# Adding expert results, layer norm and transposes inside the second attention's pipeline

## The reference, cut to what matters

```
x = x + tanh(g_xattn[0]) * L0_attention(layernorm(x), ctx)
x = x + tanh(g_ffn[0])   * L0_experts(layernorm(x))      # 16 experts, each row picks 4, plus a shared one
x = x + tanh(g_xattn[1]) * L1_attention(layernorm(x), ctx, ctx, mask)
x = x + tanh(g_ffn[1])   * L1_experts(layernorm(x))      # 8 experts, each row picks 2, plus a shared one
```

```
scores = einsum('bqghd,bkgd->bghqk', Q / 4, K) + slope * (k - q)      # 16 heads of width 16, 4 key groups
w      = softmax(where(mask, scores, lowest))
out    = einsum('bghqk,bkgd->bqghd', w, V).reshape(b, q, 256) @ Wo
```

## Time and profile before

| | us |
|---|---|
| median of 3 runs | 1741.26 (1736.82 to 1741.35) |
| profiled execution | 1740.45 |
| its span | 1738.4 |
| mean granted TensorE clock | 0.946 of 2.4 GHz |
| TensorE busy in the span | 1505.6 (87%) |
| VectorE busy | 1267.0 (73%) |
| ScalarE busy | 1046.5 (60%) |
| GpSimd busy | 794.7 (46%) |

### The profile page before, as it was taken

The page is one execution under the profiler, slowest core; times in us unless marked ns, Lnnn a source line. Parts: engine busy times, 40 slices in busy tenths (PEclk is TensorE's granted clock), DMA queues, the critical chain, the costliest instruction groups (busy, mean ns, idle before and its releaser), DMA issues. The chain is left out here.

```text
span 1738.4 us, 40154 instructions
## 1 busy us (share of the span) xinstructions
PE 1505.6 (87%) x11666; PEld 1166.6 (67%) x11666; DVE 1267.0 (73%) x4783; ACT 1046.5 (60%) x3220; POOL 794.7 (46%) x1224
## 2 busy tenths in 40 slices
PE   0499999999999999999498889991499997699998
PEld 0389888889888889888354467770366665455554
DVE  5589999999999999999576556666565554544444
ACT  4578888888888888888344345550277674222222
POOL 0766666666666666666207734441365652000000
PEclk9999999999999999999788989996599998699999
DMA  7594200000000000000116534435210000000000
GB/s 292 163 216 103 63 0 0 0 0 0 0 0 0 0 0 0 0 0 2 55 29 203 167 115 124 125 116 208 67 31 22 22 22 3 1 1 13 12 12 12
DMA packets 75226, 95.58 MB, mean 55 GB/s; under 512 B 32138, under 2 KB 60298, under 8 KB 73606
## 3 DMA queue, kind: packets, MB, share of 16 engines
q1 hardware_dynamic: 68278, 75.53, 15.1%
q0 software_dynamic: 6864, 19.01, 3.0%
HBM read 62.74 MB, written 40.43 MB: 59 GB/s over the span
## 5 line engine op out<-in xcount | busy, mean ns | idle before, releaser
L673 ACT ACTIVATE prob<-bS,ntop 128x128 f32<-128x128 f32 x512 | 181.5, 369 | 48.4 <-DVE ntop L480 48.4
L577 POOL TENSOR_TENSOR rs<-ve,half 128x6 f32<-128x6 f32 x128 | 177.3, 1385 | 0.0
L453 DVE TENSOR_SCALAR qn<-qn,mv,rs 128x128 f32<-128x128 f32 x512 | 145.9, 347 | 6.3 <-POOL rs L577 4.7
L324 PE MATMUL bS<-kT,qT 128*128 128x128 f32 x1024 | 138.3, 279 | 13.2 <-ACT prob L673 12.9
L585 POOL TENSOR_SCALAR kv<-kv,rs,nb 128x128 f32<-128x128 f32 x256 | 132.3, 522 | 27.5 <-POOL nb L580 27.5
L300 PE MATMUL bq<-w,xq 128*128 128x256 f16 x1024 | 133.8, 274 | 6.7 <-DVE xq L425 6.7
L324 PEld LDWEIGHTS bS<-kT,qT 128*128 128x128 f32 x1024 | 126.1, 194 | 16.8 <-issue 14.3
L644 ACT ACTIVATE qT<-bqT,vecs 128x256 f32<-128x256 f32 x256 | 134.9, 596 | 3.6 <-PE bqT L284 3.6
L574 POOL TENSOR_TENSOR ve<-mv,eps 128x6 f32<-128x6 f32 x128 | 34.9, 273 | 219.7 <-DVE mv L446 219.7
L341 PE MATMUL bO<-pT,kv 128*128 128x256 f32 x512 | 132.0, 380 | 1.9 <-ACT pT L657 1.9
L358 PE MATMUL bY<-wproj,catq 128*128 128x256 f16 x1024 | 132.7, 273 | 0.8 <-DVE catq L500 0.8
(11 more groups left out here) (296 smaller groups left out, 4315.2 us busy)
## 6 DMA issues: line engine op xcount, KB each, us to landing
f_xblk<-by_slot SPq DMA_DIRECT2D x79, 132.0 KB, 2.1
by_slot<-zeros SPq DMA_DIRECT2D x1, 10112.0 KB, 35.8
f_xn<-by_pick SPq DMA_DIRECT2D x16, 512.0 KB, 4.3
f_wstage<-by_expert SPq DMA_DIRECT2D x16, 480.0 KB, 3.6
l_piece<-in_f_w SPq DMA_DIRECT2D x16, 312.0 KB, 2.9
wo_stage<-in_wproj SPq DMA_DIRECT2D x8, 512.0 KB, 4.1
by_expert<-in_f_w SPq DMA_DIRECT2D x18, 128.0 KB, 2.8
x<-in_x SPq DMA_DIRECT2D x1, 2048.0 KB, 8.3
```

The lines of the kernel that those rows point to most:

```text
L324: done = nc.tensor.matmul(bS[:, h, :], qT[:, t, h, :], kT[:, t, h // HPG, :], start=True, stop=True)
L453: done = nc.vector.tensor_scalar(qn[:, off % 4, h, :], qn[:, off % 4, h, :], mv[:, t, h, 0:1], rs[:, t, h:h + 1], ALU.subtract, ALU.mult)
L577: nc.gpsimd.tensor_tensor(rs[:, t, :], ve[:], r["half"][:, 0:6], ALU.pow).then_inc(rs_ready, 1)
L673: done = nc.scalar.activation(prob[:, t, h, :], bS[:, h, :], ACT.Exp, bias=ntop[:, t, h:h + 1], scale=SCALE, accum_out=total[:, t, h:h + 1])
```

## The change

The adding loop leaves `sparse_ffn`, and the stage "a1n" is gone. `attention1` gets both:

- Before its pipeline it splits the small weights, adds the four picks of batches 0 and 1, and normalises, turns and splits batch 0.
- In the loop, while batch b is worked on, VectorE adds the picks of batch b+2 (two in step 0, two in step 1, around find_top), takes its statistics in step 2 ahead of find_top, aggregates them behind find_top, and normalises it in step 3. GpSimd computes its two small scale instructions. In batch b+1's step 0 TensorE turns batch b+2 into the upper half of the PSUM bank of V; ScalarE takes its high part at the end of step 0, VectorE its low part at the start of step 1.
- TensorE's projection of q and k moves from step 0 to step 1, ScalarE's take of it from step 1 to step 2, and VectorE's take of V from step 3 to step 2.
- The two halves of the keys are counted one by one, and TensorE waits for each where it needs it.
- SyncE fetches the picks of batch n+2 behind weight piece n, into two buffers in place of four.

```diff
@@ attention1, TensorE
+            def turn_x(b, u):
+                reach(pe, s["v_ready"], b)
+                reach(pe, x_low, b)
+                pe.wait_ge(x_normed, b + 1)
+                for k in range(KT):
+                    done = nc.tensor.transpose(bv[:, D + k * P:D + (k + 1) * P], xn[:, u, k * P:(k + 1) * P], ident)
+                done.then_inc(x_turned, 1)
...
             def score(b, u, c):
-                if c == 0:
-                    pe.wait_ge(s["kblock_ready"], b + 1)
+                if c % 2 == 0:
+                    pe.wait_ge(s["kblock_ready"], b * 2 + c // 2 + 1)
...
-                if more and c == 0:
+                if ahead and c == 0:
+                    turn_x(b + 1, 1 - u)
+                if ahead and c == 1:
                     project_qk(b + 1)
-                if more and c == 1:
                     project_v(b + 1)
@@ attention1, ScalarE
-                if more and c == 1:
+                if ahead and c == 2:
                     take_qk(b + 1, 1 - u)
                 if live(2):
                     take_pT(b, c - 2)
                 if live(0):
                     exponents(b, u, c)
+                if ahead and c == 0:
+                    take_high(b + 1)
@@ attention1, VectorE
+            def add_pick(b, u, half, k):
+                dve.wait_ge(combined if k else back_loaded[u], b * K0 + k if k else half * 16 + 16)
+                nc.vector.scalar_tensor_tensor(out=x[:, b, :], in0=back[:, u, k, :], scalar=shares[:, b, k:k + 1],
+                                               in1=x[:, b, :], op0=ALU.mult, op1=ALU.add).then_inc(combined, 1)
...
+                if ahead and c == 1:
+                    take_low(b + 1)
                 if live(0):
                     add_alibi(b, c)
+                if ahead > 1 and c < 2:
+                    add_pick(b + 2, u, half + 1, 2 * c)
...
                 if live(4) and c == 2:
                     divide(b - 1)
-                if more and c == 3:
+                if ahead and c == 2:
                     take_v(b + 1, 1 - u)
+                if ahead > 1 and c == 2:
+                    take_stats(b + 2)
                 if live(0):
                     find_top(b, c)
+                if ahead > 1 and c < 2:
+                    add_pick(b + 2, u, half + 1, 2 * c + 1)
+                if ahead > 1 and c == 2:
+                    take_moments(b + 2, u)
+                if ahead > 1 and c == 3:
+                    norm_x(b + 2, u)
@@ attention1, GpSimd
+            def x_scales(b, u):
+                pool.wait_ge(x_moments, b + 1)
+                nc.gpsimd.tensor_tensor(xve[:], xmv[:, u, 1:2], r["eps"][:, 0:1], ALU.add).then_inc(x_ve, 1)
+                pool.wait_ge(x_ve, b + 1)
+                nc.gpsimd.tensor_tensor(xrs[:, u, :], xve[:], r["half"][:, 0:1], ALU.pow).then_inc(x_rs, 1)
...
+            with pool.Fori(1, B // 2 - 1) as i:
+                x_scales(i * 2 + 1, 1)
+                keys_and_piece(i, 0)
+                x_scales(i * 2 + 2, 0)
+                keys_and_piece(i, 1)
@@ attention1, SyncE
+            def load_back(n):
+                reach(sp, combined, (n - 1) * K0)
+                sp.dma_start(back[:, n % 2].rearrange("p k d -> p (k d)"), of_token[n]).then_inc(back_loaded[n % 2], 16)
+            load_back(0)
...
+            load_back(1)
...
+            for n in range(B):
+                reach(sp, s["piece_low"], n - 1)
+                sp.dma_start(piece[:, n % 2, :], w_next[:, n * PIECE:(n + 1) * PIECE]).then_inc(piece_loaded[n % 2], 16)
+                if n + 2 < B:
+                    load_back(n + 2)
```

More of the change, by code:

```diff
@@ L974, in sparse_ffn @@
     STEPS = NC * NS
-    FETCH, BACK = 4, 4
+    FETCH = 4
     HI, LO = 0, HALF
@@ L1702, in turn_p, with step @@
                 done.then_inc(s["p_turned"], 1)
-            def step(b, u, c, live, more):
+            def step(b, u, half, c, live, ahead):
                 if live(0):
@@ L1764, in step @@
                     nc.scalar.copy(oT[:].rearrange("p a b -> p (a b)"), bY[:, 0, :]).then_inc(s["oT_ready"], 1)
+            act.wait_ge(small_loaded, 16 * len(small))
+            at = 0
+            for src, high, low in small:
+                n = src.shape[-1]
+                nc.scalar.activation(high, small_stage[:, at:at + n], ACT.Copy, scale=WS).then_inc(small_high, 1)
+                at += n
+            take_high(0)
             take_qk(0, 0)
@@ L1819, in step @@
                     nc.vector.bn_stats(r["row_stats"][:, b - 2, :], x[:, b - 2, :])
+            at = 0
+            for q, (src, high, low) in enumerate(small):
+                n = src.shape[-1]
+                dve.wait_ge(small_loaded, 16 * len(small))
+                dve.wait_ge(small_high, q + 1)
+                nc.vector.scalar_tensor_tensor(out=low, in0=small_stage[:, at:at + n], scalar=WS, in1=high, op0=ALU.mult,
+                                               op1=ALU.subtract).then_inc(small_low, 1)
+                at += n
+            for k in range(K0):
+                add_pick(0, 0, 0, k)
+            take_stats(0)
+            take_moments(0, 0)
+            add_pick(1, 1, 0, 0)
+            add_pick(1, 1, 0, 1)
+            norm_x(0, 0)
+            add_pick(1, 1, 0, 2)
+            add_pick(1, 1, 0, 3)
+            take_low(0)
+            take_stats(1)
+            take_moments(1, 1)
             take_v(0, 0)
+            norm_x(1, 1)
+            dve.wait_ge(later_loaded, 16 * len(later))
             pipeline(dve, step)
@@ new lines, in keys_and_piece @@
+            def keys_and_piece(i, u):
+                block_keys(i * 2 + u, u)
+                split_piece(i, u)
+            nc.gpsimd.memset(r["ones16"][:], 1.0)
+            pool.wait_ge(mask_loaded, 16)
+            nc.gpsimd.tensor_scalar(r["maskneg"][:].rearrange("p b s -> p (b s)"), mask[:], -1.0, 3.0e38, ALU.add,
+                                    ALU.mult).then_inc(mask_ready, 1)
+            x_scales(0, 0)
+            x_scales(1, 1)
+            keys_and_piece(0, 0)
+            x_scales(2, 0)
@@ L1852, in _ @@
+            keys_and_piece(0, 1)
+            with pool.Fori(1, B // 2 - 1) as i:
[3 more added lines that the diff above has]
+                keys_and_piece(i, 1)
+            x_scales(B - 1, 1)
+            keys_and_piece(B // 2 - 1, 0)
+            keys_and_piece(B // 2 - 1, 1)
         @block.sync
         def _(sp):
[L1854 to L1858, removed]
@@ L1863, in program @@
+            sp.dma_start(mask[:], mask_in).then_inc(mask_loaded, 16)
+            load_back(1)
+            for into, src in later:
+                sp.dma_start(into, src).then_inc(later_loaded, 16)
+            for n in range(B):
[3 more added lines that the diff above has]
+                    load_back(n + 2)
 def program(nc, t, out):
@@ L2093, in program @@
                 small.append((t[name].rearrange("p k n -> p (k n)"), flat2(r[name][0]), flat2(r[name][1])))
[L2095 to L2099, removed]
-                nc.gpsimd.memset(r["ones16"][:], 1.0)
-                pool.wait_ge(later, 48)
-                nc.gpsimd.tensor_scalar(r["maskneg"][:].rearrange("p b s -> p (b s)"), mask[:], -1.0, 3.0e38, ALU.add, ALU.mult)
+            later = ((r["wo1"][:], t["wo1"]), (r["alibi"][:], t["alibi"]))
             mf = Memory(nc, l1)
             weights = ffn_memory(mf, "f1", NT1)
-            normalise(nc, r, "a1n", None, small, load_later, early=0, finish=make_mask)
-            attention1(nc, r, t["f1_w"], weights[0])
+            attention1(nc, r, t["f1_w"], weights[0], small, later, t["mask"], by_pick, shares0)
             ffn(mf, "f1", NT1, weights, gw1, E1, E1, K1, SHARED1, False, 3, out=out)
```

118 lines of the change are left out of this document (69 added, 49 removed).

## The result

The changed kernel takes 1799.96 us (median of 4 runs, 1791.28 to 1802.05); the kernel before took 1740.99 in the same comparison. The ratio is 1.034 (95% interval 1.030 to 1.037): slower, outside the range of the prediction. Ratios compare fast executions alone; one that is over 1.5% above the fastest of its kernel counts as slow. The profiled execution has a span of 1800.0 us and a granted clock of 0.923, against 1738.4 and 0.946.

The account below looks back on a forecast made before the run. The prediction took TensorE to bound the attention loop, with two stages ahead leaving it mostly idle. Paid 55 us (50 in the loop, 5 for the clock) less 48.3 saved is 6.7 more: 1748 us, forecast's own range 1738 to 1758, overall 1724 to 1774.

Parts of the forecast that it names:

- What bounds the kernel: In the second attention's loop, TensorE is the engine the others wait for, with a period of 13.15 us.
- the new wait: Before each next batch's step 0, TensorE stands 2.1 us for keys queued behind GpSimd's scales, in 14 batches; bounds 1.7 and 2.6.
- From the first to the third score, 8.9: In each loop batch, 7.66 us now plus 0.33 for turning and 0.9 for the low part gives 8.9.
- the clock term: Low clock behind the loop's new gaps: 1.2 us each after 4 of 14, 5 us in all; bounds 0 and 17.
- Rival C: In the loop, the clock falls behind each wait, costing 17 us in place of 5: 1760; chance 0.11.
- The low part before the projection, 0.9: In the loop, VectorE's held-up norm delays the low part the projection needs: 0.3 to 1.4 us, taken as 0.9.
- TensorE's added work, 0.33 a batch: In the loop, TensorE gets two more transposes, costing 0.33 us a batch, fully paid.
- Rival D: In step 0, VectorE's adds wait for GpSimd's split, up to 1.3 us a batch, 18 us: 1766; chance 0.12.
- Saved ahead of the pipeline, 48.3: Before the loop, first scores come at 1201.9 in place of 1250.24, saving 48.3 us; bounds 44 and 51.
- the fetch's queueing: Ahead of the pipeline, the small weights queue behind the first 512 KB of the fetch, 0.3 us by estimate.

Follow-up runs that it names:

- Wait alone: Kernel before with moved projections, keys counted by halves and GpSimd's wait for step 2's negated top, without the adding work: 1833.3 us, ratio 1.052.
- wait filled: Kernel before with moved projections and GpSimd's wait, plus 18 unused matmuls where TensorE stood for the keys: 1770.6 us, ratio 1.017.
- h1_both_again: Changed kernel with statistics and moments at the end of step 1, and x turned and its high and low parts taken earlier; rerun undisturbed: 1713.6 us, ratio 0.983.
- the control: Kernel before with moved projections and keys counted by halves, without the adding stage's work or wait in the loop; run again: 1745.5 us, ratio 1.002.
- f3_lowonly: Changed kernel with x turned and its high and low parts taken earlier, statistics and moments left in step 2; beside a disturbed kernel before: 1831.0 us, ratio 1.030.
- early moments: Changed kernel with statistics and moments of batch b+2 moved from step 2 to the end of step 1: 1752.3 us, ratio 1.005.

## Why the prediction was wrong

- **What bounds the kernel, and the place of the new wait: right.** In the loop TensorE stood for the keys 13 times, 24.8 us in sum, 1.90 to 1.93 us each in the steady part (forecast 2.1, 14 times), and 7.67 us passed from the third score to the next batch (7.6).
- **From the first to the third score, 8.9: wrong,** 12.77. Not one instruction was missing from the walk; those from 1354.1 to 1364.4 ran at the lower clock. In the three batches at clock 1.00 it was 9.7.
- **The step that failed is the clock term: "I let 4 of 14 be followed by it, 5 us, with bounds 0 and 14 x 1.2 = 17".** Both halves failed. Nearly every wait was followed by the low clock (in the changed kernel three periods of 17.4 were the exceptions), and for some 10 us, not the 3.4 of the earlier trace rows. Wait alone against wait filled gives 61.3 us for it, 3.6 times the upper bound. In the changed kernel it is, by difference, 294.4 - 212.6 (the loop with neither wait) - 24.8 - 7.0 (the two waits) = 50.0 us. Rival C named the mechanism at 0.11, and the sign set down for it, a loop clock below 0.9, came (0.77); but it had the same mis-sized price.
- **Why the price was too low.** My bound took one low stretch as the price of every gap; that gap lay in another stage, with other work around it. The window of the earlier trace rows also began 1 us behind the start of that stretch and ran 1 us past its end, so even there 1.2 us should have been 1.7. And I had not looked behind the gap of 4.22 us ahead of the first score, in this very stage: the clock was low for the next 5.8 us. Both in the profile before:

```profile
921.60:925.00 3.40, 3.40 (x15) 2.06 (x16) 1.81 (x2) 0.17 (x1) 2.79 (x3) 0.50 0.95 226
1250.30:1256.10 5.80, 5.80 (x28) 3.52 (x29) 1.55 (x3) 1.56 (x9) 3.66 (x3) 0.50 0.13 27
```

- **The low part before the projection, 0.9:** in the changed kernel hardly seen, since TensorE was late itself; in the three batches at clock 1.00 it was 1.5, and with the keys' wait gone 1.6 a batch. I had priced a second chain as an addition to the first. It is a floor under it.
- **TensorE's added work, 0.33 a batch:** no run shows it alone. The floor with no wait is 14.15, not 13.48. The moved projections give 5.7 us over the loop. Of the 7 more, short waits of TensorE account for about 4 (5.6 us in h1_both_again's loop, 2.1 of them for the norm, against 1.7 in the control); the rest I can't name.
- **Rival D, the adds wait for GpSimd: wrong in its time, right in its mechanism.** In the changed kernel the adds' median is 480 ns; three of 64 took over 0.8 us, the longest 1.03, and in the steady loop the first add of a batch took 0.52, since it came when GpSimd's instruction had 0.24 us to go. Where the order put an add just behind the start of GpSimd's instruction, as in f3_lowonly, it took 1.54 us in 11 batches and ended 0.3 us after that instruction:

```profile
1376.83 1.36 POOL L1926 TENSOR_TENSOR f_w<-l_piece,f_w 128x624 f32 x1 [0.17 <-POOL l_piece L1924]
1376.94 1.54 DVE L1825 SCALAR_TENSOR_TENSOR x<-l_back,shares,x 128x256 f32 x1
```

By the Trainium skill, page "SBUF — State Buffer", section "Who interferes with whom", such instructions contend with GpSimd's reads; these rows agree.
- **Saved ahead of the pipeline, 48.3: 41.2,** below my bound of 44. The walk lacked the drain: SyncE had seen the stores at 1186.8, as counted, and the block's first instruction came at 1191.85, where the walk had 1186.9, 4.9 later. Data and split took 1.3 more; the fetch's queueing, 0.3 by my estimate, is not seen by itself.

The loop's 99.5 us are thus 17.7 without any of the waits, 24.8 and 7.0 of standing and 50.0 of clock. Less 41.2 saved, with 3.7 ahead of the change and -0.4 behind the loop, that is the 61.6 us between the spans.

## What to carry to other kernels

Where TensorE has no slack, price a new wait by where it sits: here 1.9 us of standing took another 4 by the clock in the mean of the batches, so a wait in a loop is to be designed away, or filled, before its length matters. When one wait is removed look for the next chain that was hidden by it; here the gain came only when both were gone. And what stands at a block's boundary (a drain, a barrier) is free only as long as another stage covers it.

## What the runs showed of the hardware

- Behind an idle time of 1.9 us TensorE's first score ran on at 2.4 GHz, then came 10 us of work at 1.2 GHz, in most batches; behind 1.5 us (early moments) it was 3.4 us of each 17, but in the filled version of the changed kernel waits of the same length were followed by it in only 6 of 15 batches. Work of 2.1 us in the same place, its result unused, kept the granted clock at 1.00. That a kernel gets 63 us faster (1833.3 to 1770.6) by adding matmuls was new to me.
- GpSimd's drain at the end of the block that ends in indirect DMAs takes 8.04 to 8.07 us in every profile here, counted from its own record, which begins 0.6 us ahead of that of the last issue. Where nothing else held the block (the profile after and six more), GpSimd's first instruction came 6.8 us behind the end of that issue.
- VectorE's instructions beside GpSimd's: the norm took 2.06 us beside the keys, and 0.40 in the mean of 12 with the early moments, where it began within 0.1 us of the end of GpSimd's instruction. VectorE's adds, whose two matrix inputs lie in SBUF, waited in the same way: 0.48 us by themselves, 1.54 behind GpSimd's start. The first split of the weights, 128x16, with two inputs in SBUF, took 1.79 us beside GpSimd's mask in the profile after, and 0.17 with GpSimd idle in the profile before. After, then before:

```profile
1197.70 1.79 DVE L1887 SCALAR_TENSOR_TENSOR gw<-l_small_stage,gw 128x16 f16<-128x16 f32 x1 [15.57 <-ACT gw L1785]
```
```profile
1241.12 0.17 DVE L871 SCALAR_TENSOR_TENSOR gw<-a1n_stage,gw 128x16 f16<-128x16 f32 x1
```
